# One more wait in the middle of each block's gathers, in both passes of a graph network kernel

## What is computed

```python
# layer 0: message passing
h_nodes = mlp2(h, node_W1, ...); h_edges = mlp2(edge_attr, edge_W1, ...)
msgs = mlp2(concat([h_nodes[dst], h_nodes[src], h_edges]), msg_W1, ...)
agg = segment_sum(msgs, dst) / max(counts, 1)
x = x + layernorm(h + mlp2(concat([h, agg]), upd_W1, ...))
# layer 1: attention with 4 heads
h = (relu(layernorm(x)) @ W).reshape(N, 4, 32)
e = leaky_relu(a_src[src] + a_dst[dst]); m = segment_max(e, dst)
p = exp(e - m[dst]); alpha = p / (segment_sum(p, dst) + 1e-16)
x = x + segment_sum(h[src] * alpha, dst) + bias     # self loops included
```

## Time and profile before

| | us |
|---|---|
| three runs | 6842.28, 6823.84, 6816.73 |
| median | 6823.84 |
| span of the profiled execution | 6902.9 |
| mean granted PE clock, share of full | 0.695 |
| POOL busy in the span | 2939.7 (43%) |
| PE busy in the span | 3852.3 (56%) |
| DVE busy in the span | 2513.5 (36%) |
| ACT busy in the span | 2885.9 (42%) |

### The profile page before, as it was taken

How to read it: one execution, slowest core, us unless ns; L and a number is a source line. 1 busy time by engine, 2 the same in 40 slices (tenths; PEclk the granted TensorE clock), 3 DMA queues, 4 the chain that set the end, 5 groups by cost and what they waited for, 6 DMA issues and landing times. The chain is left out here.

```text
span 6902.9 us, 129088 instructions
## 1 busy us (share of the span) xinstructions
PE 3852.3 (56%) x30843; PEld 3297.3 (48%) x30844; DVE 2513.5 (36%) x10438; ACT 2885.9 (42%) x5922; POOL 2939.7 (43%) x3114
## 2 busy tenths in 40 slices
PE   5667776767667666666724444444444444444445
PEld 3555655655556545555524444344344434434435
DVE  4321111111111233333524444444444444544446
ACT  3333333333333444444524444444444444434445
POOL 4444444444444443334254444444444444444442
PEclk8777777777776777777856666666666666666666
DMA  4111111111111111111131111111111111111111
GB/s 126 41 33 35 33 33 34 34 34 32 34 35 33 43 49 50 48 53 47 46 84 33 34 32 33 33 33 33 33 34 34 33 34 37 44 46 43 42 45 35
DMA packets 281146, 284.42 MB, mean 41 GB/s; under 512 B 101758, under 2 KB 204702, under 8 KB 280894
## 3 DMA queue, kind: packets, MB, share of 16 engines
q0 software_dynamic: 98624, 158.00, 9.3%
q1 hardware_dynamic: 101808, 82.52, 4.4%
q10 hardware_dynamic: 80462, 41.57, 2.0%
HBM read 249.61 MB, written 29.43 MB: 40 GB/s over the span
## 5 line engine op out<-in xcount | busy, mean ns | idle before, releaser
L582 POOL DMA_INDIRECT a_G<-Htab,idx x1541 | 1454.6, 944 | 1923.2 <-DVE a_GP L1694 1285.5
L582 POOL DMA_INDIRECT p_rows<-Btab,idx x1541 | 1456.1, 945 | 1804.8 <-DVE p_z L1114 1203.3
L1849 PE MATMUL a_psCD<-ident,a_csh 4*128 4x4 f32 x586 | 143.5, 313 | 1718.9 <-DVE a_csh L1582 1704.9
L1266 ACT COPY p_ST<-p_psT 128x1024 bf16<-128x1024 bf16 x293 | 298.4, 1018 | 1723.3 <-remote 916.0
L1849 PEld LDWEIGHTS a_psCD<-ident,a_csh 4*128 4x128 f32 x586 | 117.8, 249 | 1765.9 <-DVE a_csh L1582 1751.6
L1859 PE MATMUL a_psA<-a_GP,a_S 128*128 128x132 f32 x4688 | 915.5, 373 | 2.4 <-DVE a_GP L1694 2.4
L1790 ACT CAST a_S<-a_Sb 128x512 f32<-128x512 bf16 x586 | 621.3, 1132 | 646.1 <-remote 528.1
L1425 PE MATMUL p_psA<-p_msg,p_S 128*128 128x65 f32 x4688 | 719.8, 305 | 275.1 <-issue 263.5
L1859 PEld LDWEIGHTS a_psA<-a_GP,a_S 128*128 128x128 f32 x4688 | 843.3, 275 | 7.9 <-DVE a_GP L1694 2.7
L1425 PEld LDWEIGHTS p_psA<-p_msg,p_S 128*128 128x128 f32 x4688 | 677.8, 222 | 299.1 <-issue 298.2
L1114 DVE TENSOR_TENSOR p_z<-p_psZ,p_rows 128x512 f32<-128x512 f32 x293 | 200.3, 691 | 1540.6 <-remote 1081.6
(11 more groups left out here) (219 smaller groups left out, 5389.3 us busy)
## 6 DMA issues: line engine op xcount, KB each, us to landing
p_single<-Btab SPq DMA_DIRECT2D x3456, 0.2 KB
a_single<-Htab SPq DMA_DIRECT2D x3456, 0.5 KB
arena<-in_ea SPq DMA_DIRECT2D x196, 256.0 KB
p_rows<-Btab,idx POOLq DMA_INDIRECT x1541
a_G<-Htab,idx POOLq DMA_INDIRECT x1541
Htab<-u_H ACTq DMA_DIRECT2D x49, 136.0 KB, 2.0
arena<-Htab SPq DMA_DIRECT2D x7, 952.0 KB
n_x<-in_x SPq DMA_DIRECT2D x14, 448.0 KB, 4.2
```

The source lines that it names most:

```text
L582: pool.indirect_dma_start(out=rows[:, at, :], out_offset=None, in_=table, in_offset=bass.IndirectOffsetOnAxis(ap=idx[odd][:, at:at + 1], a ...
L1266: act.copy(ST[u][:, :, :], psT[:, :, :]).then_inc(s_ST, 1)
```

## The change

GpSimd waits once more within a block. The first four columns of a block are fetched when the older block in the slot has had its last step, as before. Ahead of the fifth it now waits until one more step is done, `used + 1`. The first seven blocks of a pass have `used = None` and stay as they were. `sem_inc(s_turn, 1)` counts a semaphore that nobody waits for.

```diff
         for c in range(C if whole or u < SLOTS - 1 else C - 1):
             at = u * C + c
+            if used is not None and c == C // 2:
+                pool.wait_ge(s_used, used + 1)
+                pool.sem_inc(s_turn, 1)
             pool.indirect_dma_start(
```

## The result

| | before | after |
|---|---|---|
| runs, same chip | 4 | 4 |
| lowest, median, highest, us | 6816.73, 6832.78, 6842.28 | 6324.06, 6337.72, 6347.82 |
| ratio of the times, 95% interval | | 0.9277 [0.9262, 0.9293] |
| mean granted PE clock | 0.695 | 0.707 |

What follows compares the result with a forecast made beforehand. The kernel was taken as bound by gathering under a hold plus free work. Message pass -81, last third 0 and attention -36 made -117 us: 6786 profiled, 6707 us unprofiled, range 6570 to 6850.

Steps and rivals of the forecast that it cites:

- 9.0 after the last gather: Attention pass: from a run's last gather to the end of `a_GP`, 3.4 us to `a_csh` plus 5.6 us.
- the law: Message pass: a held step costs 0.8 + (1.25 n - 0.3) + 2.1 + 0.7 us for n gathers.
- best bound: Message pass: every step follows the law, so six steps take 59.8 us, 5.6 less than before.
- worst bound: Message pass: all three between-row steps lose 2.1 us more, so six steps take 66.1 us, 0.7 more.
- Last third: Message pass with the update beside: bounds of -30 to +56 us on both sides of zero, taken as 0.
- 4 + 4: Attention pass: a pair of steps with two runs of four gathers, forecast at 20.15 us.
- I take half: Attention pass: between a gain of 72 us and nothing, the forecast took -36 us.
- GpSimd's added work: One register operation, wait and increment per block: at worst 0.3 us some 190 times a pass, hidden where GpSimd waits anyway.
- Both slower ones: Rivals: slower by attention, 6920 us, chance 0.12; slower by the update stretch, 6867 us, chance 0.06.
- the free step under a run's start: Attention pass: the step in which a run starts stays unheld, as PE's `a_psCD` gets through by 0.16 us.
- ring: Block slots fetched six blocks ahead, 99 us of cover against 11 us delay; rival that it runs dry, chance below 0.01.
- No change: Rival: each hold is paid wherever it stands, so the time stays within 34 us of 6824; chance 0.17.

Runs made afterwards that it cites:

- each half of the change: The new middle wait in the message pass alone or the attention pass alone, against the kernel before, without holds: ratios 1.0002 and 1.0005.
- the same edit: Kernel before plus a small unused GpSimd operation ahead of each block's fifth gather, no new wait: 6002.28 us with holds, 4623.16 us without.
- the late block: Kernel before with all eight gathers of a block waiting one step longer, no middle wait: 6948.18 us with holds, 4053.17 us without.

## Why the prediction was wrong

The step that failed is the release after a run of gathers. It went into the sums as a constant, 3.4 us in attention (within "9.0 after the last gather") and 2.1 us in the message pass, and it is 1.4 us after four gathers, 2.0 to 2.2 after eight and 2.6 after twelve. In attention this is the largest part of the miss. In the message pass the larger part is that I took the middle between two bounds where the steps lay at the best one or better.

**What bounds the kernel: right, with holds.** DVE's wait for "remote" was the place to look, and the law that a held step follows the number of gathers bore out: steps with eight cost what they did, and the regrouping to 4, 8, 4, 4, 8, 4 happened as written. That GpSimd's work is not the bound was right here, and would have been wrong in a launch without holds, where the kernel before takes 4051 us. Too strong was that PE's results reach the others "only when a run of gathers is over". While the sixteen gathers of the earlier trace rows run, from 5002.91 to 5022.57, DVE gets one of them, PE's sums `a_psA`, 5.0 us after these ended at 5006.74 (ACT, which waits for the same sums, 4.8 us):

```profile
5003.00 3.74 PE L1859 MATMUL a_psA<-a_GP,a_S 128*128 128x132 f32 x16
...
5011.73 0.29 DVE L1576 TENSOR_TENSOR arena<-arena,a_psA 128x132 f32 x1 [3.98 <-issue]
```

This is so in 87 of the 91 runs of fifteen and sixteen of that pass, by the median some 8 us after the sums. What waits behind the run is the next result, `a_psCD`. So the hold is a long delay of PE's signals rather than a closed door.

**Message pass, first 200 steps: forecast -81, measured -178 us.** The failed step is "no row is nearer to one end, so I take the middle". The best bound was 59.8 us for six, -185 in all, and the trace lies next to it: 1976.82 / 200 x 6 = 59.3 us. The worst bound had taken one step of 15.40 us for a property of all steps between rows. In addition "2.1 to the release" is 1.4 after four gathers: the law's 8.3 us for four should have been 7.6, and 7.67 and 7.62 stand in the six above. With it the law gives 4 x 7.6 + 2 x 13.3 = 57.0 us, which is what those six took (57.1); the mean of the pass lies 2.3 us above, in places that the law doesn't describe. That the mean meets the best bound is thus partly luck.

**Last third: forecast 0, measured -23.** Within its bounds of -30 to +56, next to the line from seven gathers.

**Attention pass: forecast -36, measured -360 us.** Three errors, all to one side; the first is the term that was sized wrong, the division of the rest is bookkeeping.
- The term "9.0 after the last gather" was read after sixteen gathers and used for four and twelve. Measured from the last gather's end to the end of `a_GP`: 6.9 after 4 + 4 (4639.51 to 4646.42), 8.1 after twelve (4596.48 to 4604.62), 7.6 after eight (4620.78 to 4628.35). From `a_csh` to the end of `a_GP` it is 5.6 us as before (4640.86 to 4646.42), so the whole difference is the release. That is 2.1 + 0.9 + 1.4 = 4.4 us for six steps, and turns 69.8 into the measured 65.4. Over 48 sixes it is another -211 us.
- "I take half" was for irregular ends of blocks and for a pause that might cost a hold of its own. There was no such cost. Had I taken the whole, with the right tails, it would have been 48 x (71.3 - 65.4) = -283 us.
- The rest, some 77 us, I named only as what would make the forecast wrong: "if PE is released in the short pauses (then it gains more)". It is not so at 1 us and it is so at 1.72 us, in 42 pauses of 48. The mean six of this pass takes 2987 / 292 x 6 = 61.4 us, below the regular 65.4, and in its last third 905.34 / 92 x 6 = 59.0. Before, too, the mean was below the regular six (3347 / 292 x 6 = 68.8 against 71), so not all of that distance is PE released in pauses; how much is wasn't measured.

**GpSimd's added work: right.** The evidence is from the launches without holds, where GpSimd is the bound: 0.3 us for each of some 190 waits would be 57 us, 1.4%, and each half of the change measures 1.000.

**The rivals.** Both slower ones are refuted: 4 + 4 is 18.07 us, so the free step under a run's start survived its 0.16 us margin, and the update stretch gained. The ring did not run dry: `p_z` waited 40.7 us for SP's signals, against 25.5 before. *No change* is what each half of the change does in a launch without holds, but for another reason than I gave it: there the gathers are the bound, and no hold exists that could be moved. The Trainium skill's "A DMA cannot be slowed by a compute op, and vice versa." (SBUF — State Buffer, "SBUF: two separate sides") had the sum at 0, and the measured ratio is 0.928 with holds, and 1.000 for each half of the change without. It may be right of the ports all the same: that the hold is one of the SBUF's ports is nowhere shown, and the signals below speak for something else.

**The range.** The bounds summed to -287 us at best, and the span fell by 557. The release had been read at two lengths, 2.1 us after eight gathers and 3.4 after sixteen, and I used each as a constant where I should have asked what it is after four. A line through the two gives 1.45, 2.1 and 2.75 us after 4, 8 and 12, or 1.95 + 1.3 + 0.65 = 3.9 us less per six steps of attention, 187 us in all. The best end would have been -287 - 187 = -474 us, 6350 us, next to the measured 6338. Part of this is luck: between the profiled executions the kernel gained 557 us, 83 more than that, and the term of 79 us, by which runs without a profile were to be shorter, measured 8 us with the change (6346.0 against 6337.7).

## What to carry to other kernels

A wait that a profile puts down to "remote" on a single core deserves a timeline before any other theory; here it led to the run of gathers. Where something is held while a kind of instruction runs, read the release for each length of the run, and cut the run with pauses longer than the release after the cut length (here 1.4 us after four gathers: pauses of 1.0 us let nothing out, those of 1.7 us nearly always did). And run the kernel before beside every experiment: the same edit gave 0.868 in one launch and 1.141 in another, because the program itself was bound by something else, the holds in one and the gathers in the other.

## What the runs showed of the hardware

**One program, two speeds.** The kernel before took 6812.99 to 6934.67 us in launches of one kind (four launches) and 4046.99 to 4059.14 in the other (five), and nothing between. One chip came up in both. What decides it isn't shown.

**Signals and registers are late, not only PE's.** In launches with holds, register moves of SP stretch. First the kernel before with holds, then the late block without (min, median and max ns; line 627 is the single loads):

```profile
L627 SPq MOVE p_single<-Btab x3456: 1/29/1387, 117.0 to 3332.2; - x192
```
```profile
L627 SPq MOVE p_single<-Btab x3456: 29/29/42, 117.1 to 1972.7; - x192
```

Counted over all register instructions of SP in the kernel before with holds, 1063 of 8224 take over 0.5 us, 84% of them between 0.69 and 0.73 us. 903 of these started in a run of gathers, 158 within 3.5 us behind one, and 2 of 3947 elsewhere. Without holds none of 8224 does. DVE has 111 such, ACT 15, and PE's own register instructions none above 0.12 us. The medians of the release (1.4, 2.0 to 2.2, 2.6, 3.3 to 3.6 us after 4, 8, 12 and 16 gathers) grow with the run, and in a long run one result of PE does come out, late. My guess is one path, on which gathers, SP's steps and PE's signals wait for each other in turns of 0.7 us, with a queue that a longer run fills further. No run isolated it, and the cause stays open.
